# Local transformer, first layer: tile 0 turned, copied and projected by itself, tiles 1 to 3 as a second group

## The reference

```
h = shift_token(x)                        # second 64 channels come from the token before
q, k, v = split(h @ wqkv)                 # 8 heads of 64
q = l2norm(q) * q_scale;  k = l2norm(k) * k_scale
q, k = rotary_xpos(q, k)
o = local_attention(q, k, v)              # windows of 64 tokens, own and previous window, masked softmax
x = x + o @ wo
h = layernorm(shift_token(x)) * ln_g + ln_b
a, g = split(h @ w1 + b1)
x = x + (a * gelu(g)) @ w2 + b2
```

## Time and profile before

| | us |
|---|---|
| median of three runs | 3523.84 |
| lowest, highest | 3522.46, 3531.91 |
| the profiled execution's own time | 3529.88 |
| its span in the profile | 3528.1 |
| TensorE busy (matmul) | 2837.1 (80%) |
| VectorE busy | 2477.9 (70%) |
| GpSimd busy | 1837.4 (52%) |
| ScalarE busy | 1755.7 (50%) |

### The profile page before, as it was taken

The page is one execution under the profiler, slowest core; times in us unless marked ns, Lnnn a source line. Parts: engine busy times, 40 slices in busy tenths (PEclk is TensorE's granted clock), DMA queues, the critical chain, the costliest instruction groups (busy, mean ns, idle before and its releaser), DMA issues. The chain is left out here.

```text
span 3528.1 us, 64431 instructions
## 1 busy us (share of the span) xinstructions
PE 2837.1 (80%) x22065; PEld 1677.4 (48%) x22143; DVE 2477.9 (70%) x4050; ACT 1755.7 (50%) x3567; POOL 1837.4 (52%) x1184
## 2 busy tenths in 40 slices
PE   3678468558999995899899994677677499999998
PEld 1111256443444442677567752223222277757774
DVE  5599646548777773677577755798699677667764
ACT  3544124134555563577467732543444277637662
POOL 3499211030111101888188822697299498729871
PEclk8699769679999997999999996899799799999999
DMA  3355000032222210112111210343144111212121
GB/s 90 82 157 148 8 7 8 0 103 73 43 40 41 41 26 23 34 42 46 29 36 41 43 25 5 115 158 110 48 166 157 37 41 41 44 24 43 40 44 39
DMA packets 176118, 202.74 MB, mean 57 GB/s; under 512 B 108358, under 2 KB 122396, under 8 KB 175388
## 3 DMA queue, kind: packets, MB, share of 16 engines
q1 hardware_dynamic: 175868, 199.41, 21.8%
HBM read 138.36 MB, written 9.44 MB: 42 GB/s over the span
## 5 line engine op out<-in xcount | busy, mean ns | idle before, releaser
L319 POOL TENSOR_TENSOR arena<-arena 128x1024 f32<-128x1024 f32 x192 | 451.4, 2352 | 61.7 <-DVE arena L336 34.3
L1446 DVE TENSOR_REDUCE causal_peak_parts<-psum 128x1 f32<-128x512 f32 (+3 forms) x608 | 375.8, 659 | 105.3 <-PE psum L1303 60.1
L2051 POOL TENSOR_TENSOR arena<-arena,w_minus_half 128x16 f32<-128x16 f32 x128 | 372.5, 2911 | 130.8 <-DVE arena L1958 130.8
L1412 ACT ACTIVATE arena<-psum 128x512 f32<-128x512 f32 (+1 forms) x608 | 303.8, 595 | 229.9 <-PE psum L1325 108.3
L1893 ACT ACTIVATE arena<-psum,arena 128x128 f32<-128x128 f32 x1024 | 277.9, 380 | 258.2 <-DVE arena L1967 258.2
L336 DVE TENSOR_TENSOR_SCAN arena<-psum,arena 128x1024 f32<-128x1024 f32 x160 | 366.0, 2289 | 28.4 <-POOL arena L319 28.4
L289 ACT ACTIVATE psum<-arena,w_A 128x1024 f32<-128x1024 f32 x192 | 214.4, 1118 | 248.9 <-DVE arena L336 211.9
L2058 POOL TENSOR_TENSOR arena<-arena 128x1024 f32<-128x1024 f32 x124 | 292.1, 2356 | 6.7 <-DVE arena L1952 6.7
L1738 PE MATMUL psum<-w_layer_wqkv,arena 128*128 128x512 f32 x512 | 259.2, 629 | 6.6 <-DVE arena L1952 5.2
L262 PE MATMUL psum<-arena,m_sel 96*128 96x512 bf16 x384 | 117.6, 388 | 181.6 <-DVE arena L351 154.8
L1963 DVE COPY arena<-psum 128x512 f32<-128x512 f32 x128 | 88.5, 691 | 240.2 <-PE psum L1750 240.2
(11 more groups left out here) (331 smaller groups left out, 6652.3 us busy)
## 6 DMA issues: line engine op xcount, KB each, us to landing
arena<-scan_rows_large SPq DMA_DIRECT2D x128, 512.0 KB, 3.7
arena<-arena SPq DMA_DIRECT2D x256, 130.0 KB, 2.5
arena<-scan_rows_small SPq DMA_DIRECT2D x128, 256.0 KB, 3.8
arena<-causal_parts SPq DMA_DIRECT2D x288, 64.0 KB
causal_parts<-arena SPq DMA_DIRECT2D x8, 768.0 KB, 5.3
arena<-Z SPq DMA_DIRECT2D x128, 32.0 KB, 1.8
arena<-Z SPq DMA_DIRECT2D x32, 128.0 KB
arena<-in_c_pads SPq DMA_DIRECT2D x4, 896.0 KB
```

The costliest lines, as they stand in the source:

```text
L319: pool.tensor_tensor(inputs[:, s % 2], b_lane[:, s % U], du(*runs[o]), ALU.mult).then_inc(input_up.sem, 1)
L1412: act.activation(PT[:, kt % 2, heads[0]:heads[0] + len(heads), lo:hi], place, ACT.Exp, scale=SCALE).then_inc(probs.sem, 1)
L1446: dve.tensor_reduce(part[:, heads[0]:heads[0] + len(heads), qt, half:half + 1].rearrange("p h a -> p (h a)"), place[:, 0:len(heads) * size ...
L2051: pool.tensor_tensor(RN[:, s4, :], SS[:, s4, :], k.minus_half[:, 0:2 * HEADS], ALU.pow).then_inc(rn_in.sem, 1)
```

## The change

The first layer turns tile 0 alone, into bank 7 in place of bank 0. ScalarE copies its 128 columns, and tile 0 is projected once `h_in` has counted one tile. On TensorE the turns of tiles 1 to 3 follow behind the projection of tile 0's values, on ScalarE the copy of their 384 columns behind the copy of those values. Tile 1's projection still waits for all four tiles (`RING`). The second layer (`units` set) keeps bank 0, one copy of all four, and the same counts to wait for.

```diff
--- before.py
+++ after.py
@@ -1508,9 +1508,10 @@
         @block.tensor
         def _(pe):
             a = attention[0].tensor(pe)
-            a.turn_first()
+            a.turn_first(range(0, 1))
             a.project_first()
             a.values_first()
+            a.turn_first(range(1, 4))
             a.project_second()
             for depth in range(2):
                 u = units[depth].tensor(pe)
@@ -1524,9 +1525,10 @@
         @block.scalar
         def _(act):
             a = attention[0].scalar(act)
-            a.copy_first()
+            a.copy_first(0, 1)
             a.square_first()
             a.take_first()
+            a.copy_first(1, 4)
             for depth in range(2):
                 u = units[depth].scalar(act)
                 after = attention[1].scalar(act) if depth == 0 else None
@@ -1650,6 +1652,8 @@
     def outputs():
         return two(5).rearrange("p (b c) -> p b c", b=2)[:, :, 0:PAIRS * (HD + 1)].rearrange("p b (h d) -> p b h d", d=HD + 1)
 
+    first_bank = 0 if units else 7
+
     def in_steps(eng, step, after={}):
 
         loops = (TILES - RING - AHEAD) // RING
@@ -1718,11 +1722,11 @@
         return part
 
     def tensor(pe):
-        def turn_first():
+        def turn_first(tiles):
             pe.wait_ge(cs_in.sem, cs_in.at(0))
-            for i in range(RING):
+            for i in tiles:
                 pe.wait_ge(z_in[i].sem, z_in[i].at(64))
-                pe.transpose(bank[0][:, i * P:(i + 1) * P], ZS[:, i, :], k.ident).then_inc(h_up.sem, 1)
+                pe.transpose(bank[first_bank][:, i * P:(i + 1) * P], ZS[:, i, :], k.ident).then_inc(h_up.sem, 1)
 
         def turn_in(i, s4, outputs):
             pe.wait_ge(z_in[s4].sem, z_in[s4].at((i - s4 + RING) * 64 // RING if isinstance(i, int) else (i - s4 + RING) * 16))
@@ -1731,7 +1735,7 @@
             pe.transpose(bank[7][:, P:2 * P], ZS[:, s4, :], k.ident).then_inc(h_up.sem, 1)
 
         def project_qk(i, s4):
-            pe.wait_ge(h_in.sem, h_in.at(max(i + 1, RING) if isinstance(i, int) else i + 1))
+            pe.wait_ge(h_in.sem, h_in.at(RING if isinstance(i, int) and (units or i) and i < RING else i + 1))
             if not (isinstance(i, int) and i == 1):
                 pe.wait_ge(cs_in.sem, cs_in.at(i - 1 if isinstance(i, int) and i == 2 else i))
             for m in range(2):
@@ -1855,10 +1859,10 @@
         return part
 
     def scalar(act):
-        def copy_first():
-            act.wait_ge(h_up.sem, h_up.at(RING))
+        def copy_first(lo, hi):
+            act.wait_ge(h_up.sem, h_up.at(hi))
             act.wait_ge(v_up.sem, v_up.at(0))
-            act.copy(HT.rearrange("p s t -> p (s t)"), bank[0]).then_inc(h_in.sem, RING)
+            act.copy(HT[:, lo:hi, :].rearrange("p s t -> p (s t)"), bank[first_bank][:, lo * P:hi * P]).then_inc(h_in.sem, hi - lo)
 
         def copy_h(i, s4):
             act.wait_ge(h_up.sem, h_up.at(i + 1))
@@ -2215,7 +2219,7 @@
                 if ahead:
                     turn(u + 1, 1 - s)
                 if after and ahead == 1:
-                    after.turn_first()
+                    after.turn_first(range(4))
                 if after and not ahead:
                     after.values_first()
                 product(u, s, 2)
@@ -2252,7 +2256,7 @@
                 if ahead:
                     affine(u + 1, 1 - s)
                 if after and ahead == 1:
-                    after.copy_first()
+                    after.copy_first(0, 4)
                 gate(u, s, 2)
             if after:
                 after.take_first()
```

## The result

The changed kernel took 3499.31 us (median of 6 runs, 3493.40 to 3509.86), the kernel before 3525.74 us (median of 6, 3519.64 to 3531.91). The ratio is 0.9935 with a 95% interval from 0.9913 to 0.9957, that is 22.9 us less (15 to 31). Timed again beside 29 runs of the kernel before (median 3520.24), five runs had a median of 3502.80 and a ratio of 0.9946 (0.9932 to 0.9960): 19.0 us less (14 to 24). The forecast was 3509.4, that is 14.4 us less, with a range from 3503 to 3520. The second timing's interval still holds the 14.4.

The account below looks back on a forecast made before the run. The start was taken as a latency chain, the loop as bound by TensorE. Shifts of 7.2 and 7.3 us sum to 14.4, taken from the three-run median 3523.84: 3509.4 us, range 3503 to 3520.

Parts of the forecast that it names:

- The start is a chain of latencies behind four loads: Start of the local transformer: engines wait for four tiles; first projection begins 9 us after tile 0 was turned.
- Tile 0: -8.61: First start: tile 0's projection moves from 1416.32 to 1407.71, ready to be turned at 1421.48, not 1430.09.
- Nothing extra is on the path, no load moves: Starts: the extra ScalarE copy and the later turns of tiles 1 and 2 hide inside the wait for tile 3.
- Tile 1 at the slow clock: First start: tile 1's projection to its square takes 3.74 us (slow), not 1.92 (fast); rotation moves by -3.6.
- Shift at the loop, 7.2 and 7.3: Loop entry in stages 6 and 8: first turns of probabilities and queries come 7.2 and 7.3 us earlier, 14.4 in all.
- the bound by GpSimd: First start: GpSimd has tile 1 ready at 1432.38 on the slow clock, allowing the loop a shift of 7.16 us.
- The loop hands the shift on unchanged to the end of the stage: Loop over tiles, bound by TensorE: passes on whatever the start gains, to the end of the stage, twice.
- the fast sum: Both starts with fast projections of tile 1: 8.6 + 9.2 = 17.8 us less, a time of 3506.
- GpSimd without slack: Rival at loop entry: the 1.8 us of slack is not met, gain 5.35 + 5.36 = 10.7 us, 3513.1; chance 0.14.
- tile 1's rotation: Rival on VectorE: tile 1's rotation ahead of tile 0's queries passes on only 3.6 us twice, 7.1, 3516.7; chance 0.09.
- Hidden: Rival in the loop: GpSimd or the loads pace it and take the gain back, 3523.8; chance 0.08.
- The slower one: Rival in the loop's first steps: TensorE stays at 1.2 GHz, costing 32.4 us in all, 3541.8; chance 0.04.

Follow-up runs that it names:

- c_after: The changed kernel without further edits, timed and profiled again beside 29 runs of the kernel before: median 3502.80 us of five runs, ratio 0.9946.

## Why the prediction was right or wrong

- *The start is a chain of latencies behind four loads.* Right, and shown by undoing one part: without the early projection the split gains nothing that can be told, with one start half of the gain comes.
- *Tile 0: -8.61.* Right to 0.1 us: turned 14.69 behind its own turn, 14.67 forecast. In the second start tile 0's projection moved from 10.7 us behind the turn to 0.8. Its queries were turned there only after 16.13 us, since the projections of tiles 1 and 2, ahead in TensorE's list, took 6.33 us.
- *Nothing extra is on the path, no load moves.* Right. Tile 3's turn stayed where its load put it.
- *Tile 1 at the slow clock.* Right: 3.72 us from its projection (1405.44) to its square at 1409.16.
- *Shift at the loop, 7.2 and 7.3.* Nearly: the mean start is 65.84 before and 59.26 changed, over eight stretches each of the same two programs, 6.6 us a start, 13.2 in all for 14.4. The second start gave its share (66.70 to 59.36, 7.3 us), the first fell short (64.99 to 59.16, 5.8). There the profiles show work at 1.2 GHz in the first step, as tile 3's projection above: in c_after, where the clock was back for the values' projection (1.02 us, not 1.91), the second turn of queries came 25.47 us behind tile 0, in the first profile 27.13 (25.6 was the bound by GpSimd).
- *The loop hands the shift on unchanged to the end of the stage.* As far as the runs show, this is the step that failed: the sum put everything behind the starts at nothing. The loop itself does hand it on (from the turn of tile 5's queries on, TensorE's timelines of the two kernels agree within 0.15 us for 220 us). The end of the layer is not the loop: TensorE waits there 2.48 us, and behind it the stretch costs 0, 1.6 or 3.3 us by the clock. In the profiles it took 1.5 us less per layer with the change, 3.0 in both. Whether the change causes this is not shown. Together with the starts that is 16.2 us; the mean spans of the four profiles each differ by 15.6 (3518.0 and 3502.4), and the interval of the timing, 14 to 24 us, holds it, but not only it.
- *The time and the range.* Two things were mis-sized besides. The median of three runs, 3523.84, was the base; 29 later runs gave 3520.24, 3.6 us lower, though the six beside the changed kernel had 3525.74. And I read the profiled execution as typical, while identical instructions ahead of the edit ended anywhere from 1393 to 1407 us in the profiles of the kernel before. A range that left 3 us below the fast sum was too narrow for medians of six with this spread. Of the 10.1 us between forecast and result, some 2 are what the profiles show beyond the sum (16.2 against 14.4), and 3.6 are the base if the 29 runs are taken for it. For the others the runs show no cause, and it stays open; the spread between executions is one possibility. 13 runs of the changed kernel average 3501.4, the five of c_after 3501.7.
- *The rivals.* GpSimd without slack would have been 10.7 us and tile 1's rotation 7.1; both measured intervals (15 to 31 and 14 to 24) exclude them as the whole effect. GpSimd was named as releaser of the second turn of queries in the changed kernel's second start, after 0.42 us of idle time. The prediction had set that down as a sign of this rival, but it is also what its own sum says, where GpSimd's slack is just used up (7.3 us). Hidden is out. The slower one is out too, though what it named is real: the clock was at 0.50 for part of the first step, and the low clock at the start costs about 2 us each.

## What to carry to other kernels

Where a stage begins with several loads in a row, let the first piece go through the chain by itself; the gain is the wait for the others less what the second piece, still late, takes back, and here that was 6.6 us a start, of 8.6 and 9.8. Ask of every pause of TensorE on the way to the end whether the clock falls behind it. That term differs from execution to execution, and no sum from one trace holds it. And before a difference of 0.5% is explained from one profile of each, compare the stretches that no edit touches.

## What the runs showed of the hardware

- The same program's routed stages ran at a granted clock of 0.54 in one execution and 1.00 in another, and everything up to stage 6 differed by up to 13.6 us between four profiles (1393.23 to 1406.81).
- TensorE paused for 2.6 to 6.3 us inside a loop where no semaphore held it, in one line, at a place that followed the number of its instructions ahead: at the same tile of stage 8 in ten profiles of four programs, elsewhere or nowhere with added products. In all seventeen cases a DMA transfer of instructions began with the pause.
- Behind the same pause of 2.48 us at the end of a layer, the same work took 64.7 us where the clock stayed at 1.00, and up to 68.0 where it fell.
- Unread products in TensorE's pauses paid: with those at the ends of the layers, 17.6 us for the kernel before and 9.5 for the changed one. Some 7 us of each go with the other pause, which these kernels did not have.
